# Edge counts in blocks of 16 targets: two blocks to a bank, one-hots three chunks at a time

## The reference

```python
def _L0_gnn_ref(feat, W1, b1, W2, b2, eps, src, dst):
    msgs = feat[src]
    neigh = jax.ops.segment_sum(msgs, dst, num_segments=feat.shape[0])
    rst = (1.0 + eps[0]) * feat + neigh
    h = jnp.maximum(rst @ W1 + b1, 0.0)
    h = h @ W2 + b2
    return h + feat
...
    qk = jax.nn.relu(qk)                     # 8 heads of 64, q scaled before
    attn = jnp.einsum('bhnm,bhmd->bhnd', qk, v)
...
xn = _layernorm(x, axis=-1)
x = x + _L0_gnn_ref(xn, ...) + _L0_mix_ref(xn[None], ...)[0]
x = x + _L0_ffn_ref(_layernorm(x, axis=-1)[None], ...)[0]      # 16 experts, top 2
```

## Time and profile before

| | |
|---|---|
| median of 3 runs | 794.92 us (793.86 to 795.14) |
| profiled execution | 788.58 us, its span 786.4 us |
| granted TensorE clock, mean over the span | 0.959 of full speed |
| TensorE busy (PE) | 713.9 us, 91% |
| VectorE busy (DVE) | 432.8 us, 55% |
| ScalarE busy (ACT) | 221.6 us, 28% |
| GpSimd busy (POOL) | 126.3 us, 16% |

### The profile page before, as it was taken

One profiled execution on the slowest core, in us unless ns is written; L12 is line 12 of the kernel. 1 busy time (PEld: TensorE's weight loads), 2 busy tenths in 40 slices (PEclk: granted clock), 3 DMA queues, 4 the chain that ended last, 5 costly groups with the idle time before them and its releaser, 6 DMA issues.

```text
span 786.4 us, 11874 instructions
## 1 busy us (share of the span) xinstructions
PE 713.9 (91%) x3591; PEld 433.7 (55%) x3592; DVE 432.8 (55%) x1360; ACT 221.6 (28%) x456; POOL 126.3 (16%) x191
## 2 busy tenths in 40 slices
PE   4888899999999999999999999999996299999935
PEld 2544455455555555555554457768784276677601
DVE  5548763378778778787744443353445323333337
ACT  2313211223223233233232033232352044334300
POOL 6054440000000000000004100020202210000054
PEclk9999999999999999999999999999998599999965
DMA  9600000064260716455277700011217595333367
GB/s 296 177 0 1 1 0 2 36 233 175 108 254 30 283 38 231 152 186 190 94 281 275 311 0 1 0 41 41 81 45 277 213 382 200 129 129 116 122 192 237
DMA packets 48881, 109.28 MB, mean 139 GB/s; under 512 B 6842, under 2 KB 6858, under 8 KB 46384
## 3 DMA queue, kind: packets, MB, share of 16 engines
q1 hardware_dynamic: 43616, 85.82, 30.2%
q0 software_dynamic: 4912, 20.60, 7.4%
q10 hardware_dynamic: 288, 2.10, 0.7%
HBM read 47.35 MB, written 61.16 MB: 138 GB/s over the span
## 4 chain that ended last, share of the span: by engine, by line
PE 81%; issue 5%; POOL 4%; DVE 3%; DMA 3%; ACT 1%; SPq 0%; POOLq 0%; ACTq 0%; DVEq 0%
PE bank L1227 12%; PE bank L1210 10%; PE bank L1318 8%; PE bank L1374 7%; PE bank L1109 7%; PE bank L1178 7%; PE bank L1146 7%; PE bank L1387 6%; PE bank L1264 6%; PE bank L1189 4%; PE bank L1249 4%; POOL arena L614 2%; PE bank L1345 2%; DMA arena<-in_wqkv 2%; DVE arena L860 1%
## 5 line engine op out<-in xcount | busy, mean ns | idle before, releaser
L860 DVE TENSOR_SCALAR arena<-iota,arena 125x128 f16<-125x128 f16 x392 | 113.2, 289 | 44.0 <-PE bank L1109 32.7
L862 DVE TENSOR_SCALAR arena<-iota,arena 125x320 f16<-125x320 f16 x392 | 120.1, 306 | 0.0
L688 ACT ACTIVATE arena<-bank 128x416 f32<-128x416 f32 (+1 forms) x120 | 62.3, 519 | 155.1 <-PE bank L1210 152.1
L892 DVE TENSOR_SCALAR arena<-bank 128x416 f32<-128x416 f32 (+1 forms) x120 | 69.1, 591 | 61.8 <-PE bank L1210 61.7
L1227 PE MATMUL bank<-arena 128*64 128x416 f32 (+1 forms) x480 | 97.2, 525 | 0.4 <-DVE arena L892 0.4
L1109 PE MATMUL bank<-arena 125*128 125x320 f16 x392 | 71.8, 301 | 8.7 <-DVE arena L862 8.5
L1178 PE MATMUL bank<-arena 128*128 128x416 f32 (+1 forms) x192 | 74.7, 538 | 2.4 <-ACT arena L629 1.4
L1318 PE MATMUL bank<-arena 128*128 128x384 f32 (+2 forms) x256 | 70.3, 430 | 0.0
L1374 PEld LDWEIGHTS bank<-arena 128*128 128x128 f32 x448 | 52.9, 197 | 20.9 <-issue 20.9
L1374 PE MATMUL bank<-arena 128*128 128x128 f32 x448 | 55.1, 283 | 10.1 <-issue 10.1
L1049 DVE COPY arena<-arena 128x1024 f32 x30 | 20.8, 694 | 75.6 <-issue 68.0
(11 more groups left out here) (213 smaller groups left out, 994.8 us busy)
## 6 DMA issues: line engine op xcount, KB each, us to landing
slots<-arena SPq DMA_DIRECT2D x6, 5376.0 KB, 17.1
slots<-arena SPq DMA_DIRECT2D x2, 5120.0 KB, 16.2
arena<-in_ew POOLq DMA_DIRECT2D x9, 1024.0 KB, 7.0
arena<-slots SPq DMA_DIRECT2D x32, 256.0 KB, 2.8
slots<-arena SPq DMA_DIRECT2D x28, 256.0 KB, 2.1
arena<-in_ew SPq DMA_DIRECT2D x5, 1024.0 KB, 20.2
arena<-in_x SPq DMA_DIRECT2D x8, 512.0 KB, 6.1
arena<-in_gw SPq DMA_DIRECT2D x2, 2048.0 KB, 15.6
```

The lines of the kernel that those rows point to most:

```text
L688: act.activation(probs[0:kt, s % NPB, 0, 0:n], bank[2 * (s % 2)][0:kt, 0:n], ACT.Relu).then_inc(p0_ready, 1)
L860: dve.tensor_scalar(ring[:, at_slot:at_slot + P], iota16[0:CE, 0:P], window_cols[:, i % WBUF, 1, k:k + 1], None, ALU.is_equal)
L862: dve.tensor_scalar(ring[:, at_slot + P:at_slot + OHW], iota16[0:CE, :], window_cols[:, i % WBUF, 0, k:k + 1], None, ALU.is_equal).then_in ...
L892: dve.tensor_single_scalar(probs[0:kt, s % NPB, 1, 0:n], bank[2 * (s % 2) + 1][0:kt, 0:n], 0.0, op=ALU.max).then_inc(p1_ready, 1)
```

## The change

The windows, or blocks, are halved to 16 targets (WD), so there are 80, with one-hots of 160 columns, and USUAL is 6 chunks for 78 of them, 2 for the one with the last two nodes, 1 for the empty last. Two windows share a bank (`window_at`), and ScalarE saves both in one instruction. VectorE no longer makes the one-hots chunk by chunk: a window has two halves (HALVES) of three chunks, and a half is two `tensor_tensor` comparisons over all three, with the ramp repeated and each chunk's number held over its row. The ring holds two windows, 12 chunks. EARLY and EVERY change with the width, so the turns of a group stay as they were. GpSimd prepares columns four windows ahead where it was two. The edge tables have 80 windows, and their minima are turned in two pieces. The checks for spare chunks are four per group and stand before four different tiles' sums, where two stood before the last tile's.

```diff
--- before.py
+++ after.py
-WD = 32
+WD = 16
 NW = NT * P // WD
 WPG = P // WD
 WCOL = NT * WD
-RING = 8
-WBUF = 4
+RING = 2
+WBUF = 8
 OHW = P + WCOL
-USUAL = [-(-EDGES * min(WD, N - w * WD) // (N * CE)) + 1 for w in range(NW)]
+RW = max(-(-EDGES * WD // (N * CE)) + 1, 1) * OHW
+USUAL = [-(-EDGES * max(0, min(WD, N - w * WD)) // (N * CE)) + 1 for w in range(NW)]
 FIRST = [sum(USUAL[:w]) for w in range(NW + 1)]
+HALVES = [sorted({0, n // 2}) for n in USUAL]
+BEFORE = [sum(len(h) for h in HALVES[:w]) for w in range(NW + 1)]
...
-        ring = at(RINGB, [RING * OHW // 2], parts=CE).bitcast(f16)
+        marks2 = at(A_T + 5000, [2 * NW], parts=CP)
+        val_f = at(A_T + 5700, [500], parts=CP)
+        ring = at(RINGB, [RING * RW // 2], parts=CE).bitcast(f16)
...
-        window_cols = at(RINGB + RING * OHW * 2, [WBUF, 2, max(USUAL)], parts=CE)
+        window_cols = at(RINGB + RING * RW * 2, [WBUF, 2, max(USUAL)], parts=CE)
...
+        def window_at(w):
+            return bank[AW[w // 2 % 2]][:, w % 2 * WCOL:w % 2 * WCOL + WCOL]
...
-        PREP, FROM, EARLY = 4, 8, 8
-        EVERY = 3.35
+        PREP, FROM, EARLY = 4, 8, 16
+        EVERY = 1.675
...
-                dve_after[made].append(("pair", w, k))
-                if w % 2 == 0 and k == USUAL[w] - 1:
-                    held = ("pair", w, k)
-                elif w % 2 == 1 and k == 0:
-                    pe_after[used(made)] += [("pair", w, k), held]
-                    act_after[used(made) + 1].append(("window", w - 1))
-                else:
-                    pe_after[used(made)].append(("pair", w, k))
+                if k in HALVES[w]:
+                    dve_after[made].append(("window", w, HALVES[w].index(k)))
+                pe_after[used(made)].append(("pair", w, k))
             if w % 2 == 1:
-                act_after[used(made) + 1].append(("window", w))
+                act_after[used(made) + 1].append(("windows", w // 2))
...
-                    pool.wait_ge(onehots_ready, FIRST[w - WBUF + 1])
+                    pool.wait_ge(onehots_ready, BEFORE[w - WBUF + 1])
...
-            for _, what, i in sorted([(start(max(w - 2, 0)), "cols", w) for w in range(NW)]
+            for _, what, i in sorted([(start(max(w - 4, 0)), "cols", w) for w in range(NW)]
...
-                    if what == "window":
-                        act.wait_ge(onehots_used, FIRST[i + 1] + (i + 1) % 2)
-                        g = i // WPG
-                        if i % WPG == 0 and g >= 2:
+                    if what == "windows":
+                        act.wait_ge(onehots_used, FIRST[2 * i + 2])
+                        g, c = 2 * i // WPG, 2 * i % WPG * WD
+                        if c == 0 and g >= 2:
                             act.wait_ge(neigh_ps, g - 1)
-                        act.activation(a_t[:, g % 2, :, (i % WPG) * WD:(i % WPG + 1) * WD],
-                                       bank[AW[i % 2]][:, 0:WCOL].rearrange("p (b d) -> p b d", b=NT),
+                        act.activation(a_t[:, g % 2, :, c:c + 2 * WD].rearrange("p b (a d) -> p b a d", a=2),
+                                       bank[AW[i % 2]][:, 0:2 * WCOL].rearrange("p (a b d) -> p b a d", a=2, b=NT),
...
-            dve.tensor_reduce(mincol[:, :], bank[AW[0]][0:2 * NW, 0:CP], X, ALU.min).then_inc(mincol_ready, 1)
+            dve.tensor_reduce(mincol[:, :], bank[AW[0]][0:NW, 0:2 * CP].rearrange("w (a p) -> w a p", a=2), X,
+                              ALU.min).then_inc(mincol_ready, 1)
...
-            def do(what, i, k=0):
-                if what == "pair":
-                    if k == 0:
+            def do(what, i, half=0):
+                if what == "window":
+                    k0 = HALVES[i][half]
+                    n = (HALVES[i][half + 1] if half + 1 < len(HALVES[i]) else USUAL[i]) - k0
+                    if half == 0:
                         dve.wait_ge(cols_ready, i + 1)
-                    q = FIRST[i] + k
-                    if q >= RING:
-                        dve.wait_ge(onehots_used, q - RING + 2)
-                    at_slot = (q % RING) * OHW
-                    dve.tensor_scalar(ring[:, at_slot:at_slot + P], iota16[0:CE, 0:P],
-                                      window_cols[:, i % WBUF, 1, k:k + 1], None, ALU.is_equal)
-                    dve.tensor_scalar(ring[:, at_slot + P:at_slot + OHW], iota16[0:CE, :],
-                                      window_cols[:, i % WBUF, 0, k:k + 1], None,
-                                      ALU.is_equal).then_inc(onehots_ready, 1)
+                    if i >= RING:
+                        dve.wait_ge(onehots_used, FIRST[i - RING] + min(k0 + n, USUAL[i - RING]))
+                    hot = ring[:, i % RING * RW + k0 * OHW:i % RING * RW + (k0 + n) * OHW].rearrange(
+                        "p (k c) -> p k c", c=OHW)
+                    for c, of in ((slice(0, P), 1), (slice(P, OHW), 0)):
+                        width = c.stop - c.start
+                        ins = dve.tensor_tensor(
+                            hot[:, :, c], iota16[0:CE, 0:width].unsqueeze(1).to_broadcast([CE, n, width]),
+                            window_cols[:, i % WBUF, of, k0:k0 + n].unsqueeze(2).to_broadcast([CE, n, width]),
+                            ALU.is_equal)
+                    ins.then_inc(onehots_ready, 1)
...
-                    pe.transpose(bank[AW[0]][0:2 * NW, 0:CP], marks2, ident[0:CP, 0:CP]).then_inc(mins_ps, 1)
+                    for a in range(2):
+                        ins = pe.transpose(bank[AW[0]][0:NW, a * CP:(a + 1) * CP], marks2[:, a * NW:(a + 1) * NW],
+                                           ident[0:CP, 0:CP])
+                    ins.then_inc(mins_ps, 1)
                 elif part == 1:
                     pe.wait_ge(mincol_ready, 1)
-                    pe.transpose(bank[NB][0:1, 0:CP], mincol[:, :], ident[0:CP, 0:CP]).then_inc(min_ps, 1)
+                    for a in range(2):
+                        ins = pe.transpose(bank[NB][0:1, a * NW:(a + 1) * NW], mincol[:, a:a + 1], ident[0:NW, 0:NW])
+                    ins.then_inc(min_ps, 1)
...
-                return pe.matmul(bank[AW[w % 2]][:, 0:WCOL], of[:, at_slot:at_slot + P],
+                return pe.matmul(window_at(w), of[:, at_slot:at_slot + P],
                                  of[:, at_slot + P:at_slot + OHW], start=start, stop=stop, skip_group_check=True)
             def count_pair(w, k):
-                if k == 0 and w >= 2:
-                    pe.wait_ge(window_saved, w - 1)
-                q = FIRST[w] + k
-                pe.wait_ge(onehots_ready, q + 1)
-                product(w, ring, (q % RING) * OHW, k == 0, k == USUAL[w] - 1).then_inc(onehots_used, 1)
+                if k == 0 and w % 2 == 0 and w >= 4:
+                    pe.wait_ge(window_saved, w // 2 - 1)
+                if k in HALVES[w]:
+                    pe.wait_ge(onehots_ready, BEFORE[w] + HALVES[w].index(k) + 1)
+                product(w, ring, w % RING * RW + k * OHW, k == 0, k == USUAL[w] - 1).then_inc(onehots_used, 1)
...
-                    pe.wait_ge(window_saved, WPG * (g + 1))
+                    pe.wait_ge(window_saved, WPG // 2 * (g + 1))
                     if g:
                         pe.wait_ge(rstt_saved, g)
                     pe.wait_ge(xn_lo_ready, NT)
-                if t == NT - 1:
-                    for w in range(g * WPG, g * WPG + WPG, 2):
-                        spare_sums(w)
+                if t >= NT - WPG and (t - NT + 1) % 2 == 0:
+                    spare_sums(g * WPG + WPG - NT + t - 1)
```

More of the change, by code:

```diff
@@ L127, in layer @@
         marks = at(A_T + 2400, [2, NW, CJ], parts=CP)
-        marks2 = at(A_T + 3700, [2 * NW], parts=CP)
-        val_f = at(A_T + 4400, [500], parts=CP)
-        ring = at(RINGB, [RING * OHW // 2], parts=CE).bitcast(f16)
+        marks2 = at(A_T + 5000, [2 * NW], parts=CP)
+        val_f = at(A_T + 5700, [500], parts=CP)
+        ring = at(RINGB, [RING * RW // 2], parts=CE).bitcast(f16)
         src_i, dst_i, hi_i, lo_i, win_i, off_i = (
@@ L210, in layer @@
         last5 = sb("last5", [CP, CJ])
-        mincol = sb("mincol", [CP, 1])
+        mincol = sb("mincol", [NW, 2])
         minrow = sb("minrow", [1, 2 * NW])
@@ L793, in _ @@
             dve.wait_ge(consts_ready, 2)
-            dve.tensor_single_scalar(win_i, dst_i, 5, op=ALU.arith_shift_right)
+            dve.tensor_single_scalar(win_i, dst_i, 4, op=ALU.arith_shift_right)
             dve.tensor_single_scalar(off_i, dst_i, WD - 1, op=ALU.bitwise_and)
@@ L828, in _ @@
             link(dve.tensor_tensor(minrow[:, NW:2 * NW], minrow[:, NW:2 * NW], minrow[:, 0:NW], ALU.subtract))
-            for of, usual in ((minrow[:, NW:2 * NW - 1], USUAL[0]), (minrow[:, 2 * NW - 1:2 * NW], USUAL[NW - 1])):
+            full = N // WD
+            for of, usual in ((minrow[:, NW:NW + full], USUAL[0]), (minrow[:, NW + full:NW + full + 1], USUAL[full]),
+                              (minrow[:, NW + full + 1:2 * NW], USUAL[NW - 1])):
```

## The result

Four runs of the changed kernel have a median of 783.14 us (780.78 to 784.08); four of the kernel before 794.76 (793.86 to 795.14). The ratio is 0.9851, with a 95% interval of 0.9827 to 0.9874: 1.5% shorter, well clear of the noise though under 2%, and 0.3 us from the forecast of 783.4. The profiled execution took 783.31 us, its span 781.5. That the total fits does not say that its terms do, so they are read one by one.

What follows compares the result with a forecast made beforehand. TensorE was taken to bound the kernel, 81% of the span; -9.2 in attention and -2.3 ahead made -11.5 us, so 777.1 profiled and 783.4 as median, 6.3 above; range 771 to 796.

Steps and rivals of the forecast that it cites:

- Step 1: Counts on TensorE: 471 products of 160 columns at 0.069 us each; attention 17.1 us less, ahead of it 4.1 less.
- the bound of 0.098: Counts on TensorE: upper bound in us for one count, the length of one weight load.
- Step 2: VectorE one-hots in attention: 1.05 us a half, giving back 7.9 us through TensorE's waits; attention net -9.2 us.
- Step 3: Ahead of attention: first counts, splits and edge tables cost 1.8 us more, clock left as is; with step 1 -2.3 us.
- Step 4: Spare checks on TensorE, ScalarE saves and GpSimd's longer window instructions cost nothing; without cover, 20 more checks 4 us.
- VectorE as the bound: Rival: VectorE bounds the attention stage; at 1.45 us a half the kernel takes 803 us; chance 0.12.
- The loads' pace: Rival: weight loads on TensorE set 0.098 us a count; -1.3 us, 793.6; chance 0.06.
- The waits: Rival: TensorE's waits for VectorE vanish as long and short pairs even out; -23 us, 772; chance 0.15.
- Ring waits: Rival: VectorE waits 0.6 us for the two-window ring in each of 18 pairs with sums; no gain, 794; chance 0.07.
- the same time: Whole kernel: outcome of no measurable change, a measurement telling 1.6 us from none; chance given as 0.09.

Runs made afterwards that it cites:

- before_look2: The kernel before, unchanged, profiled once more to look at the stretch behind the attention stage: 792.40 us.
- by_chunk: Changed kernel with a half's one-hots made chunk by chunk, six tensor_scalars in place of two tensor_tensors, 16-target blocks kept: 783.47 us.
- cols_first: Changed kernel with GpSimd making the columns of windows 0 and 1 before the first split of q and k: 777.00 us, 0.9783 of before.

## Why the prediction was right, point by point

- **Step 1, fewer columns: right.** One count more costs 0.070 to 0.073 us, forecast 0.069, and the bound of 0.098 did not apply. The stage saved 15.7 us, forecast 17.1. The 81 ns per matmul of the Trainium skill ("TensorE: Matmul & The Clock Gate", section Back-to-back issue gap) do not agree with this trace: they lie above its 0.070 to 0.073 us at 160 columns.
- **Step 2, one-hots: right.** 0.55 and 0.65 us (mean of 124 each in the stage), 1.04 a half, forecast 0.56, 0.65 and 1.05. They gave back 5.6 us, forecast 7.9. Net 10.1 against 9.2: the two misses of 1.4 and 2.3 us partly cancel.
- **Step 3, ahead of attention: mis-sized.** Forecast -2.3 us with step 1, measured +1.05 against the profile that the sum was made on. Its parts: first counts 3.38 + 0.66 against 2.74 before, +1.3 (forecast 0.5); first split 0.98 + 3.28 against 0.24 + 2.63, +1.4 (forecast 2.5); second 0.83 + 0.46 against 0.24 + 2.63, -1.6 (forecast -1.5). The waits were fair; the sentence that failed is the one that leaves the clock where it is. A fall behind the second split (1.7 us) went, and two others came (1.7 and 2.8), +2.8 in all. Some 1.2 us are not accounted for. And against before_look2, in which the old kernel also lost its clock at 71 us, the changed one starts 1.6 us earlier, near the forecast: the profile that the sum was made on was of the rarer kind, as the clocks of the other executions show.
- **Step 4, at no cost: right, for a reason worth more than the prediction gave it.** GpSimd's instructions got longer (L513 0.41 us on average, 0.24 in the earlier trace rows) at no cost. The checks cost nothing as they are spread, but the price named for losing their cover was too low: 0.2 us a check and 4 us in all, measured 0.93 to 1.53 a check and 12.5 us in the median.
- **The median.** The sum gave 777.1 for a profiled execution, the two measured took 783.31 and 781.40. Adding 6.3 us for the distance of profile and median was right for the kernel before, whose profile was among its fastest executions, and wrong as a property that the changed kernel shares: its profile stands 0.2 us from its own median. Median to median the change gave 11.6 us, forecast 11.5; profile to profile 5.3 (7.2 with the second). The total is thus partly luck.
- **The rivals.** VectorE as the bound did not come at 1.04 us a half, and came at 1.41. The loads' pace did not come. The waits did not vanish: TensorE stood still for 4.2 us of the stage, forecast about 8. Ring waits did not take the gain. Two sums there are slightly off: in the rival of the loads' pace, taking 0.2 us from each pair's wait leaves some 5.1 us given back and not 4.5, so 794.2 and not 793.6; and 0.60 + 0.15 + 0.03 is 0.78, with 0.10 for the same time.

## What to carry to other kernels

Cost a change on the path by what one more instruction adds (a run of seven against a run of three), and the engine beside it by the time from start to start, not by duration: both prices came out within a few per cent here. Where a wait on TensorE grows, add the projections behind it at the lower clock level to its price, and look at more than one profile before taking a clock as given. Spread data-dependent checks on TensorE between queued matmuls; here four in a row, beside full DMA traffic, took 6.1 us where the queue covered 3.3. And look at neighbours of the change: moving GpSimd's long splits away from VectorE's one-hots brought nearly as much as the change itself (8.7 us at the start of attention and 10.5 between medians taken apart, against 11.6).

## What the runs showed of the hardware

- **GpSimd is the one that is held in the attention stage.** One tensor_scalar on 6 columns took 2.56 us beside back-to-back one-hots, while VectorE's pace of 1.04 us a half did not change. It depends on the form of the one-hots: the same 115 GpSimd instructions of the stage were busy for 53.8 us in the changed kernel, 89.9 with the third `tensor_tensor` of each half, 33.3 with one of the two left out, and 31.2 in by_chunk, whose `tensor_scalar`s keep VectorE busy for about as long. Timeline of GpSimd in the changed kernel:

```profile
241.21 0.19 POOL L513 COPY arena<-arena 125x12 f32 x1 [0.81 <-DVE arena L868]
241.48 2.56 POOL L514 TENSOR_SCALAR arena<-arena 125x6 f32<-125x6 f32 x1
```

- **TensorE's clock after a wait is not a fixed price.** In the kernel before, the 2.63 us wait near 71 us was followed by projections at full clock in two profiles and by eight that took 5.74 us in a third, while the wait of the same length at 94 to 97 us was followed by a fall in all three (4.65 us). In cols_first a wait of 2.85 us was followed by none.

- **A register load on TensorE's sequencer slows with DMA traffic.** From SBUF it took 0.30 us at a DMA share under 0.1 and about 0.9 us at a share of 1, in both kernels; the branch behind it kept its median of 0.20 to 0.21 us.
